# A cross-attention kernel on Trainium2: merged weight transfers, the halves of Wk on other engines, the lower halves of x on VectorE, four x buffers

## The reference, cut to what matters

```python
# emb = x: 16 x 100 x 512; latent = ctx: 16 x 722 x 256; fp32 throughout
q = einsum('bte,ef->btf', emb, Wq) + bq
k = einsum('bml,le->bme', latent, Wk) + bk
v = einsum('bml,le->bme', latent, Wv) + bv
w = softmax(einsum('bte,bme->btm', q, k) / sqrt(512), axis=1)   # over the 100 tokens t
y = einsum('btm,bme->bte', w, v) + emb
out = (y - mean(y)) * rsqrt(var(y) + 1e-6) * gamma + beta       # over the 512 features
```

## Time and profile before

| | |
|---|---|
| time, median of 3 runs | 148.39 us (148.14 to 148.93) |
| profiled execution: its own time | 148.1 us |
| its span (first to last instruction) | 146.2 us |
| busy: PE, PEld | 135.7 us (93%), 129.9 us (89%) |
| busy: DVE, ACT, POOL | 115.1 us (79%), 80.8 us (55%), 77.9 us (53%) |
| mean granted TensorE clock | 0.985 |
| DMA | 37.32 MB, mean 255 GB/s |

### The profile page before, as it was taken

One profiled execution on the slowest core, in us unless ns is written; L12 is line 12 of the kernel. 1 busy time (PEld: TensorE's weight loads), 2 busy tenths in 40 slices (PEclk: granted clock), 3 DMA queues, 4 the chain that ended last, 5 costly groups with the idle time before them and its releaser, 6 DMA issues.

```text
span 146.2 us, 2983 instructions
## 1 busy us (share of the span) xinstructions
PE 135.7 (93%) x1046; PEld 129.9 (89%) x1046; DVE 115.1 (79%) x212; ACT 80.8 (55%) x283; POOL 77.9 (53%) x69
## 2 busy tenths in 40 slices
PE   6998999999799979999999999999999999999920
PEld 6887999989699878999999999999999999998900
DVE  0799989699975898677968877796887976786992
ACT  4439287269719655364848455484847537483510
POOL 0461029906330665456394835639485644649891
PEclk9999999999999999999999999999999999999985
DMA  4999739999238668496788969798896887635113
GB/s 121 312 346 420 311 106 270 355 314 411 81 107 307 210 229 296 134 400 242 246 299 306 376 231 411 252 304 309 291 315 227 300 304 226 225 134 194 72 72 143
DMA packets 11534, 37.32 MB, mean 255 GB/s; under 512 B 1536, under 2 KB 2048, under 8 KB 11520
## 3 DMA queue, kind: packets, MB, share of 16 engines
q1 hardware_dynamic: 10000, 34.90, 69.1%
q10 hardware_dynamic: 1520, 2.23, 4.2%
HBM read 33.85 MB, written 3.28 MB: 254 GB/s over the span
## 4 chain that ended last, share of the span: by engine, by line
PE 64%; DVE 15%; ACT 5%; POOL 4%; DMA 4%; issue 3%; SPq 2%; POOLq 1%; DVEq 0%; ACTq 0%
PE ps_U L397 26%; PE ps_S L383 23%; PE ps_Y L418 11%; DVE xu L654 6%; DMA xT_in<-xT 4%; PE ps_U L358 3%; DVE xT_lo L642 2%; POOL result L845 2%; POOL resid L833 2%; ACT expo L522 2%; SPq L252 1%; SPq L251 1%; PE ps_w L406 1%; ACT wkT L540 1%; DVE W_lo L739 1%
## 5 line engine op out<-in xcount | busy, mean ns | idle before, releaser
L522 ACT ACTIVATE expo<-scores,negmax 121x100 f32<-121x100 f32 x96 | 35.0, 366 | 28.0 <-DVE negmax L674 28.0
L383 PE MATMUL ps_S<-G,ctxT_in 128*121 128x100 f32 (+1 forms) x384 | 43.5, 270 | 0.3 <-DVE scores L670 0.3
L397 PEld LDWEIGHTS ps_U<-prob,ctx_in 121*128 121x128 f32 x360 | 42.2, 192 | 0.9
L397 PE MATMUL ps_U<-prob,ctx_in 121*128 121x100 f32 x360 | 42.5, 274 | 0.0
L383 PEld LDWEIGHTS ps_S<-G,ctxT_in 128*121 128x121 f32 (+1 forms) x384 | 41.9, 185 | 0.6 <-issue 0.6
L838 POOL TENSOR_TENSOR rstd<-vareps,neg_half 128x1 f32<-128x1 f32 (+1 forms) x13 | 12.4, 956 | 23.5 <-DVE vareps L712 23.2
L822 POOL TENSOR_TENSOR prob<-expo,rinv 121x600 f32<-121x600 f32 x16 | 19.0, 1190 | 9.0 <-DVE rinv L681 9.0
L833 POOL TENSOR_TENSOR resid<-x_in,wkT 128x512 f32<-128x512 f32 (+1 forms) x13 | 16.6, 1279 | 13.3 <-issue 8.9
L670 DVE TENSOR_TENSOR scores<-ps_S,c_rows 121x600 f32<-121x600 f32 x16 | 12.5, 781 | 12.4 <-issue 10.9
L685 DVE TENSOR_REDUCE probsum<-prob 121x100 f32<-121x600 f32 x16 | 19.8, 1238 | 2.5 <-POOL prob L822 2.2
L522 ACT ACTIVATION_READ_ACCUMULATOR expo<-scores,negmax 121x1 f32 x96 | 18.0, 188 | 0.0
(11 more groups left out here) (92 smaller groups left out, 184.7 us busy)
## 6 DMA issues: line engine op xcount, KB each, us to landing
ctx_in<-ctx SPq DMA_DIRECT2D x16, 768.0 KB, 5.1
ctxT_in<-ctxT SPq DMA_DIRECT2D x16, 722.0 KB, 5.5
xT_in<-xT SPq DMA_DIRECT2D x8, 400.0 KB, 6.8
x_in<-x SPq DMA_DIRECT2D x12, 256.0 KB, 4.6
out<-result ACTq DMA_DIRECT2D x8, 256.0 KB, 4.5
wqT<-WqT SPq DMA_DIRECT2D x4, 256.0 KB, 3.5
out<-result SPq DMA_DIRECT2D x3, 256.0 KB, 2.0
wkT<-WkT SPq DMA_DIRECT2D x4, 128.0 KB, 3.7
```

The costliest lines, as they stand in the source:

```text
L383: last = nc.tensor.matmul(ps_scores(c)[0:rows(c), :], ctxT_in[:, q, l * M + c * MP:l * M + c * MP + rows(c)], G[:, l, bass.ds(b * T, T)], ...
L397: last = nc.tensor.matmul(ps_U[:, q, l * T:(l + 1) * T], ctx_in[0:rows(c), q, c, l * P:(l + 1) * P], prob[0:rows(c), q, c * T:(c + 1) * T] ...
L522: last = nc.scalar.activation(expo[0:MP, q, c * T:(c + 1) * T], scores[0:MP, q, c * T:(c + 1) * T], ACT.Exp, bias=negmax[0:MP, q, c:c + 1] ...
```

## The change

The two weights and the two biases are packed on the host in one array, `Wqk`, with 776 columns in each row (512 of Wq, 256 of Wk, bk twice, bq, five of nothing), and come in four DMAs of 388 KB instead of eight of 256 and 128 KB and two small ones. `wkT`, `wqT` and `bq_col` are views of the one buffer. In the weights loop ACT makes `wk_hi` for chunks 1 to 3 (DVE for chunk 0), DVE makes all `wk_lo` instead of POOL, and DVE's sum over bq is moved out of the loop to behind `u_col`. PE does the four hi·lo matmuls of a chunk before it waits for `wq_lo`. `lower_half(2)` and `lower_half(3)` go from POOL to DVE, behind `weigh_by_u(1)` and behind `lower_shift(1)`. `xT_in` has four buffers, so that SP issues all eight DMAs of x without a wait, the last two ahead of the ctxT of batch 1. The buffers `bvw`, `resid` and `result` of the token tiles lie in spent buffers of x.

```diff
-        NX = 3
-        xT_in = sb("xT_in", [P, NX, EC, GT])
+        xT_in = sb("xT_in", [P, NG, EC, GT])
+        wqk = sb("wqk", [P, EC, Wqk.shape[2]])
@@ SP
             for c in range(EC):
-                sp.dma_start(wqT[:, c, :], WqT[c]).then_inc(w_in[c], 16)
-                sp.dma_start(wkT[:, c, 0:L], WkT[c]).then_inc(w_in[c], 16)
+                sp.dma_start(wqk[:, c, :], Wqk[c]).then_inc(w_in[c], 16)
             load_group(0)
             load_group(1)
             load_ctxT(0, 0)
             load_group(2)
+            load_group(3)
             load_ctxT(1, 1)
-            sp.wait_ge(xTlo_set, 2)
-            sp.wait_ge(xu_step, EC)
-            load_group(3)
@@ PE, for each chunk f
+                wait_upper_wk(pe, f)
                 pe.wait_ge(wqhi_set, f + 1)
-                pe.wait_ge(wkhi_set, f + 1)
...
                 pe.wait_ge(wklo_set, f + 1)
-                pe.wait_ge(wqlo_set, f + 1)
...
+                pe.wait_ge(wqlo_set, f + 1)
...
@@ ACT
-                act.dma_start(bk_in[:, :], bk.rearrange("(p c) -> p c", c=EC)).then_inc(bk_loaded, 16)
-                act.dma_start(bq_col[:, :], bq.rearrange("(p c) -> p c", c=EC)).then_inc(bq_loaded, 16)
             for f in range(EC):
-                act.wait_ge(w_in[f], 32)
+                act.wait_ge(w_in[f], 16)
+                if f > 0:
+                    nc.scalar.activation(wk_hi[:, f, :], wkT[:, f, :], ACT.Copy).then_inc(wkhi_set, 1)
                 nc.scalar.activation(wq_hi[:, f, :], wqT[:, f, :], ACT.Copy).then_inc(wqhi_set, 1)
@@ DVE
             for c in range(EC):
-                dve.wait_ge(w_in[c], 32)
-                nc.vector.tensor_copy(wk_hi[:, c, :], wkT[:, c, :]).then_inc(wkhi_set, 1)
+                dve.wait_ge(w_in[c], 16)
+                if c == 0:
+                    nc.vector.tensor_copy(wk_hi[:, c, :], wkT[:, c, :]).then_inc(first_wkhi_set, 1)
+                wait_upper_wk(dve, c)
+                nc.vector.tensor_tensor(wk_lo[:, c, :], wkT[:, c, :], wk_hi[:, c, :].bitcast(F32), ALU.subtract).then_inc(wklo_set, 1)
                 dve.wait_ge(wqhi_set, c + 1)
                 nc.vector.tensor_tensor(wq_lo[:, c, :], wqT[:, c, :], wq_hi[:, c, :].bitcast(F32), ALU.subtract).then_inc(wqlo_set, 1)
-                if c == 0:
-                    dve.wait_ge(bq_loaded, 16)
-                    nc.vector.tensor_scalar(wkq[:, 0, :], wkT[:, 0, :], bq_col[:, 0:1], None, ALU.mult).then_inc(wkq_step, 1)
...
...
+            weigh_by_bq()
             lower_half(1)
...
             weigh_by_u(1)
+            lower_half(2)
             maxima(0, 0)
             lower_shift(1)
+            lower_half(3)
             weigh_by_u(2)
@@ POOL
-            for c in range(EC):
-                pool.wait_ge(w_in[c], 32)
-                pool.wait_ge(wkhi_set, c + 1)
-                nc.gpsimd.tensor_tensor(wk_lo[:, c, :], wkT[:, c, :], wk_hi[:, c, :].bitcast(F32), ALU.subtract).then_inc(wklo_set, 1)
-            lower_half(2)
-            lower_half(3)
```

More of the change, by code:

```diff
@@ L28, with xattn @@
 MC_CHUNKS = 6
-def xattn(nc, xT, x, ctxT, ctx, WqT, WkT, bq, bk, Wv, bv, gamma, beta, out):
+def xattn(nc, xT, x, ctxT, ctx, Wqk, Wv, bv, gamma, beta, out):
     B, T, E = x.shape
@@ L192, in xattn @@
         result_set = sem("result_set")
+        wqT = wqk[:, :, 0:E]
+        wkT = wqk[:, :, E:E + L + 2]
+        bq_col = wqk[:, :, E + L + 2]
         wq_hi = wq_parts[:, 0, :].rearrange("p (f e) -> p f e", e=E)
@@ L196, in xattn @@
         U_hi = wq_parts[:, :, 0:B * T]
[L197 removed]
+        spare = xT_in.rearrange("p g c t -> p g (c t)")
+        bvw = spare[:, 0, 0:2 * E].rearrange("p (q e) -> p q e", e=E)
+        resid = spare[:, 1, 0:2 * E].rearrange("p (q e) -> p q e", e=E)
+        result = spare[:, 2, 0:2 * E].rearrange("p (q e) -> p q e", e=E)
         y = wv_in
@@ L244, in exists, with wait_upper_wk @@
             return 0 <= b < B
+        def wait_upper_wk(engine, c):
+            if c == 0:
+                engine.wait_ge(first_wkhi_set, 1)
+            else:
+                engine.wait_ge(wkhi_set, c)
         block = stack.enter_context(nc.Block())
@@ L336, in _ @@
                                      start=False, stop=False)
+                pe.wait_ge(wqlo_set, f + 1)
+                for e in range(EC):
                     last = nc.tensor.matmul(banks[e][:, 0:L + 2], wq_lo[:, f, e * P:(e + 1) * P], wk_hi[:, f, :],
@@ L620, in _, with weigh_by_bq @@
             nc.vector.memset(neg_half[:, :], -0.5).then_inc(consts_set, 1)
-            dve.wait_ge(bk_loaded, 16)
-            nc.vector.tensor_copy(wkT[:, :, L:L + 2], bk_in[:, :].unsqueeze(2).to_broadcast([P, EC, 2])).then_inc(bkcol_set, 1)
-            dve.wait_ge(bkcol_set, 1)
             for c in range(EC):
-                dve.wait_ge(w_in[c], 32)
-                nc.vector.tensor_copy(wk_hi[:, c, :], wkT[:, c, :]).then_inc(wkhi_set, 1)
+                dve.wait_ge(w_in[c], 16)
+                if c == 0:
+                    nc.vector.tensor_copy(wk_hi[:, c, :], wkT[:, c, :]).then_inc(first_wkhi_set, 1)
+                wait_upper_wk(dve, c)
+                nc.vector.tensor_tensor(wk_lo[:, c, :], wkT[:, c, :], wk_hi[:, c, :].bitcast(F32), ALU.subtract).then_inc(wklo_set, 1)
                 dve.wait_ge(wqhi_set, c + 1)
                 nc.vector.tensor_tensor(wq_lo[:, c, :], wqT[:, c, :], wq_hi[:, c, :].bitcast(F32), ALU.subtract).then_inc(wqlo_set, 1)
-                if c == 0:
-                    dve.wait_ge(bq_loaded, 16)
-                    nc.vector.tensor_scalar(wkq[:, 0, :], wkT[:, 0, :], bq_col[:, 0:1], None, ALU.mult).then_inc(wkq_step, 1)
[L632 to L635, removed]
+            def weigh_by_bq():
+                for c in range(EC):
+                    if c == 0:
+                        nc.vector.tensor_scalar(wkq[:, 0, :], wkT[:, 0, :], bq_col[:, 0:1], None, ALU.mult).then_inc(wkq_step, 1)
+                    else:
+                        dve.wait_ge(wkq_step, c)
+                        nc.vector.scalar_tensor_tensor(wkq[:, c % 2, :], wkT[:, c, :], bq_col[:, c:c + 1],
+                                                       wkq[:, (c - 1) % 2, :], ALU.mult, ALU.add).then_inc(wkq_step, 1)
             banks = [ps_S[:, 0, :], ps_S[:, 1, :], ps_U[:, 0, :], ps_U[:, 1, :]]
@@ L649, in weigh_by_u @@
                     dve.wait_ge(xulo_set, g)
-                nc.vector.tensor_scalar(xu[:, 0, :], xT_in[:, g % NX, 0, :], u_col[:, 0:1], bb_col[:, 0:1],
+                nc.vector.tensor_scalar(xu[:, 0, :], xT_in[:, g, 0, :], u_col[:, 0:1], bb_col[:, 0:1],
                                         ALU.mult, ALU.add).then_inc(xu_step, 1)
@@ L653, in weigh_by_u @@
                     dve.wait_ge(xu_step, EC * g + e)
-                    nc.vector.scalar_tensor_tensor(xu[:, e % 2, :], xT_in[:, g % NX, e, :], u_col[:, e:e + 1],
+                    nc.vector.scalar_tensor_tensor(xu[:, e % 2, :], xT_in[:, g, e, :], u_col[:, e:e + 1],
                                                    xu[:, (e - 1) % 2, :], ALU.mult, ALU.add).then_inc(xu_step, 1)
@@ L845, in finish @@
                 nc.gpsimd.tensor_tensor(result[0:n, q, :], scaled[0:n, q, :], beta_rows[0:n, :], ALU.add).then_inc(result_set, 1)
[L847 to L854, removed]
             def turn(b, q):
```

32 lines of the change are left out of this document (13 added, 19 removed).

## The result

The changed kernel takes 145.92 us (median of 4 runs, 145.61 to 146.08). Its ratio to the kernel before is 0.984 (95% interval 0.9822 to 0.9859), a gain of 2.1 to 2.6 us. The profiled executions took 148.1 and 146.08 us, their spans are 146.2 and 144.3, so the traces hold 1.9 to 2.0 us of it. 147.8 had been forecast, in a range from 146.7 to 148.9.

What follows compares the result with a forecast made beforehand. It took x's arrival, then VectorE's path to group 2's shift sum, to set when TensorE's unbroken run begins. Gain 1.1 - 0.5 = 0.6 us: profiled 148.1 to 147.5, median forecast 147.8, range 146.7 to 148.9.

Steps and rivals of the forecast that it cites:

- TensorE's unbroken run: TensorE busy in every microsecond from 56.6 to 135.4 us; forecast to begin 0.6 us earlier, the shift arriving whole at the end.
- the 4.6 us off weigh_by_u(1): VectorE's three steps for group 1, forecast to fall from 6.56 to 1.97 us with POOL idle.
- the 1.7 for the sum over bq: Time forecast to be added to VectorE's path by the bq sum, now behind u_col and ahead of lower_half(1): 1.7 us.
- part 1: Weights stage: merged weight DMAs bring x's first group 1.1 us earlier, within bounds of 0 and 1.9.
- rival 1: Weights stage: x arrives as much earlier as it is issued, at 8.7; gain 1.4 us, time 147.0; chance 0.20.
- Rival 3: Weights stage: bytes bind, x still arrives at 10.6, VectorE's longer path shows alone; time 148.9; chance 0.17.
- The cover of W: Weights stage: W ready by 10.6 us, x's upper halves done at 11.3, so 0.7 us in hand.
- A: Time from the span's start to the arrival of x's first group: 10.6 us before, forecast 9.5.
- part 2: VectorE's path from x's arrival to group 2's shift sum, forecast to grow 0.5 us, from 27.6 to 28.1.
- the wait ahead of maxima(0): VectorE's wait of 1.16 us for ScalarE to take the shift; forecast 0.5 left, 0.65 off.
- the two pairs of lower halves: lower_half(2) and lower_half(3), moved onto VectorE's path, forecast to add 2.0 us each.
- part 3: SP's queue: its wait of 10.1 us goes, but nothing waited for the transfers behind it, so nothing is won.

## Why the prediction was wrong

That TensorE's unbroken run is only shifted, and that the shift arrives whole, was right (2.0 at the third shift sum, 2.0 at 53.04). So were the 4.6 us off weigh_by_u(1) (6.56 to 1.98), the 1.7 for the sum over bq (1.84 from 13.43 to lower_half(1) at 15.27), and lower_shift(2) (1.55 for 1.64). Three terms were not.

**The arrival of x (part 1).** I took 1.1 of the 1.9 us; in this trace all 1.9 came (10.6 to 8.7, the figure of rival 1). I had let the time from x's issue to its landing grow from 6.03 to 6.8 us; it was 6.0. In the other six traces with the same DMAs it was 5.9 to 6.9, so my 1.1 (landing at 9.5) lies at the late end of what comes. Rival 3, by which x gains nothing, is out. The ground, the length of the rows, holds by the run with short rows, but the rate expected (near 400) was not reached in the stretch.

**The cover of W.** I had W ready 0.7 us ahead of x's upper half at A = 9.5, and just in time at 8.7. It came 0.86 late: TensorE's product is bound by itself from 5.33 (the first chunk 2.1 us, then 1.43 each) and ends at 11.4. Of the 1.9 us project(0) got 0.96. But VectorE, whose path mattered, got more: lower_half(0) now ends before W_hi and no longer stands in front of W_lo, so W_lo starts at 11.83 where it started at 13.44 behind lower_half(0). The lead there is 1.6. The timeline of the kernel before, for the comparison:

```profile
11.52 2.00 DVE L642 TENSOR_TENSOR xT_lo<-xT_in,xT_hi 128x800 fp32r<-128x800 f32 x2
...
12.91 1.69 PE L358 MATMUL ps_Y<-xT_hi,W_hi 128*128 128x400 f32 x8 [0.42 <-ACT W_hi L576]
...
13.44 0.75 DVE L739 SCALAR_TENSOR_TENSOR W_lo<-ps_S,W_hi 128x256 fp32r<-128x256 f32 x2
...
15.03 1.88 DVE L642 TENSOR_TENSOR xT_lo<-xT_in,xT_hi 128x800 fp32r<-128x800 f32 x2
```

**VectorE's path (part 2), the step that failed by most.** I summed +0.5 from x's arrival to the shift sum. From the end of u_col, which is free of the start's change, it ran 15.11 to 38.24 before, 23.1 us, and 13.51 to 36.22 after, 22.7: it shrank by 0.4, where the sum implies 23.6. Two terms were mis-sized. One is the wait ahead of maxima(0). I left 0.5 of its 1.16, with ScalarE's five steps at 5.6 us; they took 4.9 (20.24 to 25.17), since neighbouring instructions of one engine overlap at their ends (two upper halves 1.61, not 1.75), and under 0.1 was left: 0.45 us. The other is the two pairs of lower halves, at 2.0 each. A pair took 1.89, and overlaps its neighbours too, so that it put only 1.8 us (group 2) and 1.7 us (group 3) on the path: 0.5 together. lower_shift(2) gave 0.1, and the sum over bq took 0.15 more than I had: 0.45 + 0.5 + 0.1 - 0.15 = 0.9. TensorE still waited ahead of the shift sum, but 0.28 and not the 1.3 that I had named.

Together 1.6 + 0.4 = 2.0, where I had 1.1 - 0.5 = 0.6.

**SP's queue (part 3), wrong and hidden by the change itself.** "Nothing waited for it, so nothing is won" was true of the kernel before and false of one that is 2 us faster: the changed kernel wants ctxT of batch 2 at 36.7, and in the four traces with three buffers it landed at 36.9 to 38.2. The run with three buffers shows 1.7 us lost, some two thirds of it to ctxT and the rest to x's last group. I looked for waits on DMAs, and not for how near a landing was to its use.

**The edits do not add.** Undone one by one from the changed kernel they cost 0.9 (merge), 2.3 (lower halves), 1.7 (four buffers) and nothing (Wk's halves), 4.9 in all against 2.4. In the kernel before three limits lay within a microsecond of each other: VectorE's path (the shift sum at 38.24), ctxT of batch 2 (landed at 37.9) and TensorE's own work (done at 37.42), which begins with project(0) and so with W and x. A sum of the edits' own terms, as I made it, can't show that.

## What to carry to other kernels

Where an engine or a transfer is the limit, list the next two with their distance in microseconds (a landing against its first use, too) before pricing an edit: how far one edit pays is set by them, and several edits must be costed together. Add durations of neighbouring instructions from rows with "x2" or "x3", not from single ones. An engine's lead gained early is spent by the first step that is moved into its path: look there for what eats it, as the sum over bq did when the lower halves stayed on POOL.

## What the runs showed of the hardware that I had not expected

The first weight transfers ran at 320 to 375 GB/s (seven traces) for rows of 3104 bytes on 128 partitions. They ran at 294 for rows of 2048 and 1056 bytes, at 290 for rows of 1552, and at 262 for rows of 3104 on 64 partitions in twice the DMAs (one trace each). The busy share of the DMA engines was 0.93 to 0.99 in all of them. Cutting a DMA by partitions cost more than cutting it by columns, in SP's issues (0.6 against 0.43 us) and in the rate; why is open.

A product of 121x6 elements on VectorE took 1.54 us beside POOL's residual and 0.17 alone. In the changed kernel:

```profile
31.79 0.17 DVE L686 TENSOR_TENSOR rinv<-rall,mask 121x6 f32<-121x6 f32 x1
...
51.08 1.54 DVE L686 TENSOR_TENSOR rinv<-rall,mask 121x6 f32<-121x6 f32 x1
51.34 1.26 POOL L836 TENSOR_TENSOR xT_in<-x_in,xT_in 128x512 f32<-128x512 f32 x1
```

It ended with POOL's instruction (52.62 and 52.60): beside POOL a tiny instruction can cost as much as what POOL has in hand. Two of VectorE's instructions with one input in SBUF, the on-chip memory that holds all of these tiles but the `ps_` ones, were not slowed: the sum `probsum` took 1.27 us beside Wv_lo and 1.23 with POOL idle, and `scores`, which reads `ps_S` and `c_rows`, took 0.77 beside POOL's beta at 52.82 and 0.78 with POOL idle at 25.36. That agrees with the Trainium skill, page "SBUF — State Buffer", section "SBUF: two separate sides", by which a VectorE instruction with two SBUF inputs and a GpSimd one that reads SBUF exclude each other for the whole instruction. Moving the lower halves off POOL, so that VectorE's steps no longer met them, was worth 2.3 us here; letting U_lo run ahead of the stalled product was worth 0.6 to 0.9.
